# The seam behind the feed-forward stage: where the second tanh, the last gelu and the token outputs stand

## Chip, cores, metric

One core of one Trainium2 chip runs the whole kernel. The metric is the device time in microseconds of one execution; lower is better. TensorE (PE in the rows) multiplies, ScalarE (ACT) evaluates functions, VectorE (DVE) and GpSimd (POOL) do elementwise work, SyncE (SP) issues the DMAs.

## What is computed

64 batches of 256 tokens by 256 features pass through one cross-attention (16 heads of 16, 120 keys) and a coupling network that is applied three times. Cut to what matters:

```python
# attention: query = layernorm(x), key = value = ctx
u = einsum('hbqd,hbkd->hbqk', q, k) * scale / sqrt(d_k)
logits = where(mask, -inf, tanh(u) * exp(log_C))
x = x + (softmax(logits) @ v, heads joined) @ W_out.T

# feed-forward: out = layernorm(x)
gf = global_net(out.mean(axis=1))
for _ in range(3):
    h = gelu(out @ w1 + b1)          # 256 -> 256
    h = gelu(h @ w2 + b2)            # 256 -> 128
    h = gelu(h @ w3 + b3)            # 128 -> 64
    tf = sigmoid(h @ w4 + b4)        # one number per token
    coupling = 0.1 + adaptive_range * (0.7 * gf + 0.3 * tf - 0.5) * 2.0
    out = out + coupling * twist(out)
x = x + out
```

Sigmoids are computed as tanh of half the argument.

## The kernel before

Each engine runs its own program, written out by hand in the order in which it is to run, and waits on semaphores for the others. All of them walk through the same list of stages (`slots()`): attention slots i = -2, -1, 0, ..., and after every eighth batch one feed-forward stage for the eight batches that are then ready (`GROUP` = 8, 8 stages). In attention slot i batches of different age are worked on at once: scores, tanh and exp of batch i; weighted values of batch i-1; queries and keys of batch i+1; the output projection of batch i-2; normalised features of batch i-3 (`LAG` = 3).

Scores and probabilities of a batch come in two halves n = 0 and 1 of eight heads. `scores(b, n)` (L1184) fills four banks of PSUM, `tanh(b, n)` (L939, 120 x 2048 elements) reads them, and the next scores may overwrite them only behind that tanh. `exp(b, n)` (L945) works in place in SBUF; `weighted_values(b, n)` (L1200) multiplies the result with the values.

A feed-forward stage has twelve passes p = 0 to 11 (three cycles of four chunks, two batches to a chunk; `PASSES` = 12, `UPDATES` = 8). A pass is layer 1 and `gelu1` (L973), `layer2` (L1294) and `gelu2` (L997), `layer3` (L1303) and `gelu3` (L1009), and then, in passes 0 to 7, `layer4` and `tanh4`, and in passes 8 to 11 `token_output` (L1334): two columns for each 128 tokens, collected over the four passes. `token_tanh` (L1027) reads the sixteen columns together; `coefficients` on GpSimd (L498) waits for it. `layer3(p)` waits for `gelu3(p-1)`, since all passes use one bank for it.

Eight banks of PSUM: 0 to 3 scores, 4 weighted values, 5 side products, 6 transposes of queries, keys and features (`TR_BANK`), 7 the projection (`X_BANK`). In the feed-forward stage layer 2 uses 4 and 5, and layer 3 uses the first half of bank 6. The token outputs of before lie in bank 6 too, from column 288 (`TOKEN_AT`).

What is called the seam here is the end of a feed-forward stage and the attention slot behind it. Its batch is e = 11, 19, ..., 59 (`early` in the code): seven seams; behind the eighth stage only the end of the program follows. The stage takes work of slot e ahead: TensorE issues `scores(e, 0)` in round p = 10 of its last loop, `scores(e, 1)` in round 11 and `weighted_values(e-1, 0)` in round 12. ScalarE has `tanh(e, 0)` behind `gelu3(9)` and `tanh(e, 1)` behind `gelu3(10)`; `gelu3(11)`, the token tanh, a table load and `exp(e, 0)` follow, then `features(e-3)` (L955), which copies transposed features out of bank 6. In slot e, `queries(e+1)` (L1159) waits for the token tanh, because it overwrites bank 6. On VectorE `attn_out` (L717) transposes weighted values, `queries_out` (L703) and `keys_out` (L708) copy queries and keys out of bank 6, and `residual` (L742) adds the projection.

Each float32 matmul of the code appears in the rows as two MATMULs, so that 8 of them are x16.

## Time and profile before

| what | us |
|---|---|
| median of 3 runs | 1058.44 |
| lowest, highest run | 1058.36, 1059.02 |
| the profiled execution, its own time | 1058.27 |
| its span, from the first to the last instruction | 1056.40 |
| TensorE busy | 974.1 (92%) |
| ScalarE busy | 899.3 (85%) |
| VectorE busy | 818.9 (78%) |
| GpSimd busy | 604.4 (57%) |

The busy shares are averages over stages with different limits. Whether an engine is what the others wait for is read from the idle times before its instructions and from what ended them. All times below count from the start of the span. The rows of a timeline give start, duration, engine, line and operation, what is written and read, how many instructions are merged (x), and, in brackets, the idle time of the engine before the first of them with the instruction that ended it.

### The profile page before, as it was taken

Reading aid. Unit: us, or ns where it says so; the run is one execution under the profiler, and the core shown is the slowest. Engines: PE = TensorE matmul, PEld = TensorE weight load, DVE = VectorE, ACT = ScalarE, POOL = GpSimd, SP = SyncE. Lnnn points to the kernel's source line nnn. Section 1 sums busy time; section 2 is a strip of 40 time slices with the busy share of each in tenths; the row PEclk is TensorE's granted clock in tenths of the full one; section 3 lists DMA queues with packets and bytes.
Section 4 is the critical chain, followed back from the end, with each engine's and each line's share of the span. In section 5 each row is a group of like instructions: output and inputs, shape, how many; then the busy total and the mean of one; then the engine's idle time right before and its main releaser. Section 6 shows DMA issues by size and latency. Waiting matters only on the chain.

```text
span 1056.4 us, 21739 instructions
## 1 busy us (share of the span) xinstructions
PE 974.1 (92%) x7260; PEld 529.3 (50%) x7260; DVE 818.9 (78%) x1655; ACT 899.3 (85%) x1121; POOL 604.4 (57%) x1077
## 2 busy tenths in 40 slices
PE   5899999999999999999999999999999999997993
PEld 4556435564356544565445653556435654454432
DVE  3888785997869876887869978599786887687475
ACT  3899878997899978998789987899789997896575
POOL 3366715887069850898328980588706975087204
PEclk7999999999999999999999999999999999999897
DMA  5433001430023300332005310153002430021002
GB/s 119 89 60 60 6 2 31 118 89 1 2 69 91 78 1 1 90 92 57 2 1 119 89 30 1 30 119 90 0 2 70 94 75 1 1 49 38 11 1 80
DMA packets 191117, 51.70 MB, mean 49 GB/s; under 512 B 165920, under 2 KB 174624, under 8 KB 191008
## 3 DMA queue, kind: packets, MB, share of 16 engines
q1 hardware_dynamic: 191008, 50.31, 22.1%
q8 instruction: 60, 0.98, 0.4%
q14 instruction: 49, 0.40, 0.1%
HBM read 33.37 MB, written 16.78 MB: 47 GB/s over the span
## 4 chain that ended last, share of the span: by engine, by line
PE 46%; ACT 37%; issue 10%; POOL 3%; SPq 2%; DVE 1%; DMA 1%; ACTq 0%; POOLq 0%; DVEq 0%
ACT probs L939 17%; PE ps L1294 15%; ACT probs L945 13%; PE ps L1280 8%; PE ps L1264 6%; PE ps L1303 5%; ACT f_t L955 4%; PE ps L1184 4%; PE ps L1215 3%; PE ps L1200 2%; ACT h L997 1%; PE ps L1324 1%; ACT h L973 1%; PE ps L1334 1%; SPq L412 1%
## 5 line engine op out<-in xcount | busy, mean ns | idle before, releaser
L939 ACT ACTIVATE probs<-ps,u_scale 120x2048 f32<-120x2048 f32 x128 | 258.0, 2015 | 21.2 <-PE ps L1184 20.4
L945 ACT ACTIVATE probs<-probs,exp_bias,clip 120x2048 f32<-120x2048 f32 x128 | 275.6, 2153 | 0.1
L1294 PE MATMUL ps<-h,w 128*128 128x512 f32 x384 | 185.7, 606 | 9.9 <-ACT h L973 8.7
L1184 PE MATMUL ps<-q_t,k_t 32*120 32x256 f32 x2048 | 148.2, 403 | 26.7 <-ACT probs L939 25.9
L717 DVE STREAM_TRANSPOSE o_t<-ps 128x512 f32<-128x512 f32 x128 | 90.6, 708 | 71.5 <-PE ps L1200 71.2
L1215 PE MATMUL ps<-wo_t,of_t 128*128 128x256 f32 x512 | 143.5, 403 | 1.0 <-DVE xy L742 1.0
L498 POOL TENSOR_SCALAR tok_c<-tok_c,c_tok 128x32 f32<-128x32 f32 x8 | 2.3, 288 | 241.6 <-issue 241.6
L1200 PE MATMUL ps<-probs,va 120*32 120x256 f32 x2048 | 138.8, 389 | 1.3 <-ACT probs L945 1.3
L1184 PEld LDWEIGHTS ps<-q_t,k_t 32*120 32x120 f32 x2048 | 93.8, 179 | 63.8 <-issue 59.5
L1215 PEld LDWEIGHTS ps<-wo_t,of_t 128*128 128x128 f32 x512 | 86.9, 189 | 50.0 <-issue 41.7
L1294 PEld LDWEIGHTS ps<-h,w 128*128 128x128 f32 x384 | 67.5, 189 | 87.9 <-issue 58.4
L479 POOL TENSOR_SCALAR f_hat<-xy,neg,rstd 128x256 f32<-128x256 f32 x128 | 102.6, 808 | 13.3 <-POOL rstd L469 13.3
L557 POOL TENSOR_TENSOR f_hl<-f_t,f_hl 128x512 f16<-128x512 f32 x64 | 83.2, 1311 | 35.6 <-DVE f_hl L764 35.6
L973 ACT ACTIVATE h<-f_t,b 128x512 f32<-128x512 f32 x144 | 95.6, 714 | 6.8 <-DVE f_t L827 5.5
L997 ACT ACTIVATE h<-ps,b 128x512 f32<-128x512 f32 x96 | 65.7, 684 | 40.9 <-PE ps L1294 40.9
L458 POOL TENSOR_SCALAR q_hat<-xy,neg,rstd 128x256 f32<-128x256 f32 x128 | 88.1, 696 | 11.0 <-POOL rstd L448 10.5
L1280 PE MATMUL ps<-f_hl,w_hl 128*128 128x512 f16 x384 | 92.6, 385 | 0.0
L802 DVE SCALAR_TENSOR_TENSOR move_u<-coup,r_batch,v_t 128x512 f32<-128x512 f32 x64 | 45.9, 758 | 48.0 <-ACT coup L1021 47.1
L1200 PEld LDWEIGHTS ps<-probs,va 120*32 120x32 f32 x2048 | 53.8, 110 | 56.8 <-ACT probs L945 18.4
L539 POOL TENSOR_SCALAR twisted<-xy,neg,b_r 128x256 f32<-128x256 f32 x112 | 70.5, 637 | 1.2 <-POOL x_add L498 1.1
L1264 PE MATMUL ps<-f_hl,w1t_hl 128*128 128x512 f16 x288 | 68.8, 379 | 0.1
L1303 PE MATMUL ps<-h,w 128*64 128x256 f32 x384 | 62.6, 404 | 3.5
(138 smaller groups left out, 1766.0 us busy)
## 6 DMA issues: line engine op xcount, KB each, us to landing
xy<-in_x_dram SPq DMA_DIRECT2D x64, 256.0 KB, 3.4
out_dram<-xy SPq DMA_DIRECT2D x64, 256.0 KB, 2.0
cbuf<-in_ctx_dram SPq DMA_DIRECT2D x64, 120.0 KB, 2.8
va<-in_ctx_dram SPq DMA_DIRECT2D x64, 120.0 KB, 3.6
tok_c<-coup SPq DMA_DIRECT2D x256, 0.5 KB, 2.0
move_v<-in_L_xattn_W_out_dram SPq DMA_DIRECT2D x1, 256.0 KB, 5.2
move_u<-in_L_ffn_cn_w_dram SPq DMA_DIRECT2D x1, 256.0 KB, 3.3
w<-in_L_ffn_cn_w_dram SPq DMA_DIRECT2D x1, 128.0 KB, 3.1
```

What stands on the lines that cost most here:

```text
L479: eng.tensor_scalar(f_hat[:, t, :], xy[:, at, t * E:(t + 1) * E], neg2[:, at, t:t + 1], rstd2[:, at, t:t + 1], ALU.add, ALU.mult).then_inc ...
L717: eng.transpose(o_t[:, b % 2, 2 * n:2 * n + 2].rearrange("p c q r -> p (c q r)"), banks(PV_BANK)).then_inc(s_ot, 1)
L939: eng.activation(probs[:, b % 2, n * HALF:(n + 1) * HALF, :].rearrange("k h q -> k (h q)"), banks(SCORE_BANK, 4)[0:KEYS, :], ACT.Tanh, sca ...
L945: eng.activation(p, p, ACT.Exp, scale=clip[0:KEYS, 0:1], bias=exp_bias[:, b:b + 1]).then_inc(s_exp, 1)
L973: eng.activation(h1[:, p % 2, m, :], source, ACT.Gelu, bias=b1[:, m:m + 1], scale=by) \
L1184: last = eng.matmul(banks(SCORE_BANK + r)[0:KEYS, odd * S:(odd + 1) * S], k_t[rows, b % 2, odd, n, :], q_t[rows, b % 2, n, :], start=True, ...
L1200: last = eng.matmul(banks(PV_BANK)[j * SLOT:(j + 1) * SLOT, (c % 2) * S:(c % 2 + 1) * S], va[:, b % VR, h, :], probs[:, b % 2, h, :], star ...
L1215: last = eng.matmul(banks(X_BANK)[:, t * E:(t + 1) * E], of_t[:, k, t * P:(t + 1) * P], wo_t[:, k, :], start=(k == 0), stop=(k == EK - 1))
L1264: last = eng.matmul(banks(V_BANKS[m]), w1t_hl[:, w, k, m * P:(m + 1) * P], halves[:, f, k, :], start=(n == 0), stop=(n == len(PRODUCTS) - 1))
L1280: last = eng.matmul(banks(U_BANKS[m]), w1_hl[:, w, k, m * P:(m + 1) * P], halves[:, f, k, :], start=(n == 0), stop=(n == len(PRODUCTS) - 1))
L1294: last = eng.matmul(banks(bank), w2[:, k, :], h1[:, p % 2, k, :], start=(k == 0), stop=(k == EK - 1))
L1303: last = eng.matmul(banks(L3_BANK)[b * M3:(b + 1) * M3, 0:S], w3[:], h2[:, p % 2, b * S:(b + 1) * S], start=True, stop=True, tile_position ...
```

## The change

In the feed-forward stage, ScalarE runs only `tanh(e, 0)` ahead; `tanh(e, 1)` goes into slot e, between `exp(e, 0)` and `features(e-3)`, so `gelu3(11)` stands ahead of it, directly behind `gelu3(10)`. TensorE issues `layer3(11)` ahead of the token outputs of pass 10, and moves `scores(e, 1)` and `weighted_values(e-1, 0)` from the stage into slot e. The token outputs lie in bank 7 at column 0. `queries(e+1)` waits for `gelu3(11)` instead of the token tanh, and the projection in slot e waits for the token tanh instead of the last `tanh4`. Slot e on TensorE has another order, and on VectorE it begins with `queries_out(e+1)`. Slots other than e keep their order.

```diff
-        TOKEN_AT = S + 32
+        TOKEN_BANK = X_BANK
...
+                    if after_ffn(i) and nxt < NB:
+                        queries_out(nxt)
                     if 0 <= here < NB:
                         attn_out(here, 0)
-                    if 0 <= nxt < NB:
+                    if 0 <= nxt < NB and not after_ffn(i):
                         queries_out(nxt)
...
                     if 0 <= i < NB:
                         exp(i, 0)
+                    if i < NB and first:
+                        tanh(i, 1)
...
                             gelu3(i, p - 1)
-                            if early < NB and p >= PASSES - 2 and p < PASSES:
-                                tanh(early, p - PASSES + 2)
+                            if early < NB and p == PASSES - 2:
+                                tanh(early, 0)
...
                 elif after_ffn(b - 1):
-                    eng.wait_ge(s_ttok, groups_before(b - 1))
+                    eng.wait_ge(s_h3, PASSES * groups_before(b - 1))
...
                     if after_ffn(b + 2):
-                        eng.wait_ge(s_th, UPDATES * groups_before(b + 2))
+                        eng.wait_ge(s_ttok, groups_before(b + 2))
...
-                    at = TOKEN_AT + t * GROUP + chunk * CB
-                    last = eng.matmul(banks(TR_BANK)[:, at:at + CB], h3[:, p % 2, t * P:(t + 1) * P],
+                    at = t * GROUP + chunk * CB
+                    last = eng.matmul(banks(TOKEN_BANK)[:, at:at + CB], h3[:, p % 2, t * P:(t + 1) * P],
...
-                        if p - 2 >= UPDATES:
+                        if p - 2 >= UPDATES and p < PASSES:
                             token_output(i, p - 2)
                         if p - 1 < PASSES:
                             layer3(i, p - 1)
+                        if p >= PASSES:
+                            token_output(i, p - 2)
...
-                        if early < NB:
-                            if p == PASSES - 2:
-                                scores(early, 0)
-                            if p == PASSES - 1:
-                                scores(early, 1)
-                            if p == PASSES:
-                                weighted_values(early - 1, 0)
+                        if early < NB and p == PASSES - 2:
+                            scores(early, 0)
```

TensorE at the first seam, before. `h` is the output of a gelu, L1294 layer 2, L1303 layer 3, L1334 the token outputs of one pass, L1184 scores, L1200 weighted values, L1215 projection, L1159 queries, L1168 keys, L1228 features:

```order
L1294 MATMUL ps<-h,w 128x512 x2
L1334 MATMUL ps<-w4rep,h 128x2 x2
L1303 MATMUL ps<-h,w 64x256 x2
L1184 MATMUL ps<-q_t,k_t 120x256 x8
L1334 MATMUL ps<-w4rep,h 128x2 x2
L1303 MATMUL ps<-h,w 64x256 x2
L1200 MATMUL ps<-probs,va 32x256 x8
L1334 MATMUL ps<-w4rep,h 128x2 x2
L1215 MATMUL ps<-wo_t,of_t 128x256 x2
L1159 MATMUL ps<-ident,q_hat 128x128 x4
L1200 MATMUL ps<-probs,va 32x256 x8
L1168 MATMUL ps<-ident,cbuf 128x120 x2
```

Behind these come the second projection, the features and the scores of batch e+1. The same place on TensorE in the changed kernel, whose lines stand 4 further down (L1298 is layer 2, L1307 layer 3, L1338 token outputs, L1188 scores, L1204 weighted values, L1219 projection, L1163 queries, L1172 keys, L1232 features):

```order
L1298 MATMUL ps<-h,w 128x512 x2
L1338 MATMUL ps<-w4rep,h 128x2 x2
L1307 MATMUL ps<-h,w 64x256 x4
L1338 MATMUL ps<-w4rep,h 128x2 x4
L1188 MATMUL ps<-q_t,k_t 120x256 x8
L1163 MATMUL ps<-ident,q_hat 128x128 x4
L1204 MATMUL ps<-probs,va 32x256 x8
L1172 MATMUL ps<-ident,cbuf 128x120 x2
L1219 MATMUL ps<-wo_t,of_t 128x256 x2
L1204 MATMUL ps<-probs,va 32x256 x8
L1232 MATMUL ps<-ident,f_hat 128x128 x4
L1219 MATMUL ps<-wo_t,of_t 128x256 x2
```

The two layer 3 stand together, and so do the last two token outputs; a block of scores and one of weighted values have moved from ahead of the last token outputs to behind them.

ScalarE at the same seam, before (L997 is gelu2, L1009 gelu3, L939 tanh, L945 exp, L1027 the token tanh, L955 features):

```order
L939 ACTIVATE probs<-ps,u_scale 120x2048
L997 ACTIVATE h<-ps,b 128x512
L1009 ACTIVATE h<-ps,b 128x256
L939 ACTIVATE probs<-ps,u_scale 120x2048
L1009 ACTIVATE h<-ps,b 128x256
L1027 ACTIVATE tok_th<-ps,half_b 128x16
L945 ACT_TABLE_LOAD
L945 ACTIVATE probs<-probs,exp_bias,clip 120x2048
L955 ACTIVATE f_t,f_sum<-ps 128x256 x2
L939 ACTIVATE probs<-ps,u_scale 120x2048
```

And in the changed kernel, where each of these lines stands 2 further down:

```order
L941 ACTIVATE probs<-ps,u_scale 120x2048
L999 ACTIVATE h<-ps,b 128x512
L1011 ACTIVATE h<-ps,b 128x256 x2
L1029 ACTIVATE tok_th<-ps,half_b 128x16
L947 ACT_TABLE_LOAD
L947 ACTIVATE probs<-probs,exp_bias,clip 120x2048
L941 ACTIVATE probs<-ps,u_scale 120x2048
L957 ACTIVATE f_t,f_sum<-ps 128x256 x2
L941 ACTIVATE probs<-ps,u_scale 120x2048
```

The second tanh has moved from between the last two gelus to behind the exp.

## Rows read from the trace of the kernel before

**Rows 1.** The page: shares of the chain that ended last, by engine, by line.

```profile
PE 46%; ACT 37%; issue 10%; POOL 3%; SPq 2%; DVE 1%; DMA 1%; ACTq 0%; POOLq 0%; DVEq 0%
ACT probs L939 17%; PE ps L1294 15%; ACT probs L945 13%; PE ps L1280 8%; PE ps L1264 6%; PE ps L1303 5%; ACT f_t L955 4%; PE ps L1184 4%; PE ps L1215 3%; PE ps L1200 2%; ACT h L997 1%; PE ps L1324 1%; ACT h L973 1%; PE ps L1334 1%; SPq L412 1%
```

**Rows 2.** Waits of ScalarE, 171.9 to 297.3 us: us in total, times, longest us.

```profile
ACT probs L939 <- PE ps L1184: 0.9, 2, 0.6
```

**Rows 3.** Timeline of ScalarE, first seam: start, duration, instruction, idle before.

```profile
167.47 0.47 ACT L1009 ACTIVATE h<-ps,b 128x256 f32<-128x256 f32 x1 [0.24 <-PE ps L1303]
168.56 1.97 ACT L939 ACTIVATE probs<-ps,u_scale 120x2048 f32<-120x2048 f32 x1 [0.61 <-PE ps L1184]
170.43 0.47 ACT L1009 ACTIVATE h<-ps,b 128x256 f32<-128x256 f32 x1
171.59 0.27 ACT L1027 ACTIVATE tok_th<-ps,half_b 128x16 f32<-128x16 f32 x1 [0.70 <-PE ps L1334]
...
173.18 2.10 ACT L945 ACTIVATE probs<-probs,exp_bias,clip 120x2048 f32<-120x2048 f32 x1
...
176.92 1.97 ACT L939 ACTIVATE probs<-ps,u_scale 120x2048 f32<-120x2048 f32 x1 [0.26 <-PE ps L1184]
178.79 2.08 ACT L945 ACTIVATE probs<-probs,exp_bias,clip 120x2048 f32<-120x2048 f32 x1
```

**Rows 4.** Timeline of TensorE, the same stretch.

```profile
166.77 0.65 PE L1303 MATMUL ps<-h,w 128*64 128x256 f32 x4
167.35 1.14 PE L1184 MATMUL ps<-q_t,k_t 32*120 32x256 f32 x16
...
170.95 0.61 PE L1334 MATMUL ps<-w4rep,h 128*128 128x2 f32 x4 [0.33 <-ACT h L1009]
171.41 1.11 PE L1215 MATMUL ps<-wo_t,of_t 128*128 128x256 f32 x4
172.36 0.60 PE L1159 MATMUL ps<-ident,q_hat 128*128 128x128 f32 x4
172.89 1.07 PE L1200 MATMUL ps<-probs,va 120*32 120x256 f32 x16
173.89 0.42 PE L1168 MATMUL ps<-ident,cbuf 120*128 120x120 f32 x2
174.15 1.03 PE L1215 MATMUL ps<-wo_t,of_t 128*128 128x256 f32 x4
175.16 0.63 PE L1228 MATMUL ps<-ident,f_hat 128*128 128x128 f32 x4
175.71 1.14 PE L1184 MATMUL ps<-q_t,k_t 32*120 32x256 f32 x16
```

**Rows 5.** Timeline of ScalarE, second seam: the tanh of the next slot.

```profile
302.42 1.97 ACT L939 ACTIVATE probs<-ps,u_scale 120x2048 f32<-120x2048 f32 x1 [0.26 <-PE ps L1184]
```

**Rows 6.** Timeline of all engines, end of the eighth feed-forward stage.

```profile
1038.44 0.47 ACT L1009 ACTIVATE h<-ps,b 128x256 f32<-128x256 f32 x1 [0.24 <-PE ps L1303]
...
1038.97 0.61 PE L1334 MATMUL ps<-w4rep,h 128*128 128x2 f32 x4 [0.57 <-ACT h L1009]
...
1039.50 0.65 PE L1303 MATMUL ps<-h,w 128*64 128x256 f32 x4
1040.20 0.47 ACT L1009 ACTIVATE h<-ps,b 128x256 f32<-128x256 f32 x1 [1.29 <-PE ps L1303]
...
1040.73 1.01 PE L1334 MATMUL ps<-w4rep,h 128*128 128x2 f32 x4 [0.57 <-ACT h L1009]
1041.78 0.27 ACT L1027 ACTIVATE tok_th<-ps,half_b 128x16 f32<-128x16 f32 x1 [1.10 <-PE ps L1334]
```

**Rows 7.** Timeline of VectorE, first seam: the copy of the queries.

```profile
173.00 0.69 DVE L703 COPY q_t<-ps 128x512 f32<-128x512 f32 x1 [1.60 <-PE ps L1159]
```

**Rows 8.** Windows in the tail: PEclk is the granted clock as a share.

```profile
1040.20:1040.60 0.40, 0.00 (x0) 0.00 (x0) 0.00 (x0) 0.40 (x1) 0.00 (x0) 0.95 0.00 0
1040.60:1041.00 0.40, 0.27 (x2) 0.27 (x2) 0.00 (x0) 0.08 (x1) 0.00 (x0) 0.50 0.00 0
```

More of the change, by code:

```diff
@@ L1026, in token_tanh @@
                 eng.wait_ge(s_coef, COEFS * g)
-                eng.activation(tok_th[:], banks(TR_BANK)[:, TOKEN_AT:TOKEN_AT + GT], ACT.Tanh, scale=0.5,
+                eng.activation(tok_th[:], banks(TOKEN_BANK)[:, 0:GT], ACT.Tanh, scale=0.5,
                                bias=half_b4[:, 0:1]).then_inc(s_ttok, 1)
@@ L1371, in _ @@
                             project(old, 0)
-                    else:
-                        if old < NB:
-                            project(old, 0)
+                        if 0 <= nxt < NB:
+                            keys(nxt)
+                        if 0 <= here < NB:
+                            weighted_values(here, 1)
+                        if 0 <= old < NB:
+                            project(old, 1)
+                        if 0 <= i - LAG < NB:
+                            norm_to_features(i - LAG)
+                    else:
+                        if i < NB:
+                            scores(i, 1)
                         if nxt < NB:
@@ L1377, in _ @@
                         if here < NB:
-                            weighted_values(here, 1)
-                    if 0 <= nxt < NB:
-                        keys(nxt)
-                    if 0 <= here < NB and i != early:
-                        weighted_values(here, 1)
-                    if 0 <= old < NB:
-                        project(old, 1)
-                    if 0 <= i - LAG < NB:
+                            weighted_values(here, 0)
+                        if nxt < NB:
+                            keys(nxt)
+                        if old < NB:
+                            project(old, 0)
+                        if here < NB:
+                            weighted_values(here, 1)
                         norm_to_features(i - LAG)
+                        if old < NB:
+                            project(old, 1)
                     if i == 0:
```

## The prediction

> **What bounds the kernel now.** I read the page's chain of waits first. TensorE holds 46% of it and ScalarE 37%, and the two largest single lines of it are the tanh and the matmuls of layer 2 [rows 1]. In the stretch between two seams (from behind the token tanh of the first to the one of the second) ScalarE waits for scores only twice, 0.9 us in all [rows 2]. One attention slot after another therefore runs from one ACTIVATE to the next: whatever moves the start of tanh(e+1,0), the first tanh of the slot behind the seam, moves everything after it. Here e is the batch whose scores the feed-forward stage takes ahead: 11, 19, ... 59, so there are seven seams; the eighth stage has none.
>
> So I look at what sets that tanh. In the timeline of ScalarE across the first seam there are idle times of 0.24, 0.61, 0.70 and 0.26 us in the rows shown, each ended by TensorE [rows 3]. The last, before tanh(12,0) at 176.92, was ended by the scores of batch 12, whose matmuls began at 175.71. In the timeline of TensorE these stand at the end of an unbroken file: token outputs at 170.95, which had waited 0.33 us for the last gelu, then projection, queries, weighted values, keys, projection, features, scores [rows 4]. That file is the path; the exp and the table load on ScalarE lie beside it. In the second seam the same tanh starts at 302.42, which is 125.50 us later, one whole group of eight batches; the seams repeat [rows 5].
>
> **The change part by part: the tanh and its scores.** Before, tanh(e,1) stood between gelu3(10) and gelu3(11). It started at 168.56, so the last gelu couldn't run before 170.43 [rows 3]. That tanh is now behind exp(e,0), and its scores (1.07 us of TensorE, 167.35 to 168.42) behind the last token outputs [rows 4]. The last layer 3 no longer has to follow scores and token outputs. It waits for gelu3(10), because that gelu reads the same bank. Gelu3(10) started at 167.47 [rows 3]; from the start of such a gelu to the TensorE instruction that waits for it are 0.53 us (1038.44 to 1038.97, in the tail) [rows 6]. So layer3(11) starts at 168.00. From its start to the start of its gelu are 0.70 us where TensorE had just worked (166.77 to 167.47, 1039.50 to 1040.20) [rows 3, 4, 6]. Here it comes out of an idle time of 0.58 us (layer3(10) began at 166.77 and took 0.65). Token outputs behind an idle time handed over after 0.53 us (1038.97 to 1039.50), those behind work after at most 0.47; so I add 0.05, between nothing and 0.10, and have gelu3(11) start at 168.75. Token outputs of pass 11 then start 0.53 later at 169.28, against 170.95: 1.67 us earlier. The token tanh follows 0.64 later (170.95 to 171.59) at 169.92, also 1.67 earlier.
>
> The Trainium skill has a rule on that addition: the page TensorE: Matmul & The Clock Gate, section "Single matmul latency", says that an isolated matmul shows its drain while one in a stream hides it. By that rule the 0.70 would be 0.80 here, and the sum 0.05 us a seam higher than mine; the token rows agree in direction (0.53 against 0.47).
>
> **TensorE behind the token outputs.** Before, the file from 170.95 to the scores at 175.71 was 4.76 us. The new file has all of it, plus two blocks that used to lie in the shadow of ScalarE's tanh: scores(e,1), 1.07 us, and weighted_values(e-1,0). The latter's price is that of its twin, 172.89 to 173.89, 1.00 us. Step by step, start to start [rows 4]: token outputs 0.46, scores 1.07, queries 0.53, weighted values 1.00, keys 0.26, projection 0.98 (0.95 and 1.01 are there), weighted values 1.00, features 0.55, projection 0.98. The sum is 6.83 us. 169.28 + 6.83 = 176.11, against 175.71: the scores of batch 12 start 0.40 us **later**, and tanh(12,0) with them, at 177.32. The gain of 1.67 us at the token outputs is eaten by 2.07 us of matmuls that lost their cover. Six of the junctions (such as features to projection) don't occur in the trace; the junctions that do differ by a few hundredths, so I allow 0.10 us either way.
>
> What else lies in the file's way: queries need their bank free, and that is now told by gelu3(11), over at about 169.2, before their 170.81. Keys need the queries' copy on VectorE: 0.64 us after the start of the queries (172.36 to 173.00) plus its 0.69 [rows 4, 7], so 172.14, against the keys' turn at 172.34. That is 0.20 us of slack, and it is there because the copy now goes ahead of the transpose of o_t. Projection waits for the token tanh, which is long over. ScalarE: exp at 171.51 (1.59 behind the token tanh, as before, with a table load between), tanh(11,1) at 173.61 if the exp takes its 2.10, its end at 175.58 [rows 3]. The scores of 12 overwrite its banks and must wait for it, and TensorE gets there at 176.11: 0.5 us of slack. So TensorE's file is still what comes last. The coefficients on GpSimd start 1.67 us earlier, and VectorE's queue is less crowded, but neither ends a wait of tanh(12,0); nothing is taken from that.
>
> **The tail.** The eighth stage has no scores in it, only layer3(11) in front of token outputs(10). Before: 1038.97, 1039.50, gelu 1040.20, token outputs 1040.73, token tanh 1041.78 [rows 6]. Now layer3(11) starts at 1038.97, gelu3(11) at 1039.72, token outputs at 1040.25. Their way to the tanh is 0.64 us at 2.4 GHz (the seam) and 1.05 us at 1.2 GHz (1040.73 to 1041.78); the clock fell between 1040.2 and 1040.6 [rows 8]. So the token tanh comes at 1040.89 or 1041.30, 0.89 or 0.48 us earlier. I take 0.7. The chain behind it (coefficients, twisted parts, stores) is unchanged.
>
> **The sum.** 7 x 0.40 = 2.8, less 0.7, is +2.1 us. With the allowances (7 x 0.10 and 0.2 for the tail) it is +1.2 to +3.0. The profiled execution took 1058.27 us, of which 1056.40 is its span; the median of the runs is 1058.44, 0.17 above. On the profile's own time the sum gives 1060.4, on the median 1060.5.
>
> **Rivals.** (1) ScalarE's order becomes the path and the gain is kept. If TensorE's blocks pack closer than the rows show, scores(12,0) wait for tanh(11,1) alone. With an exp step of 2.00 (its 2.10 less the 0.10 by which a tanh overlaps the next ACTIVATE, 176.92 + 1.97 against 178.79 [rows 3]) that ends at 175.48, scores 0.05 later, 0.2 us before the old 175.71. Then 7 x -0.2 and the tail's -0.7 give -2.1: 1056.3. Against it: 0.5 us would have to vanish from nine steps read in this same seam.
> (2) TensorE's clock falls in the seam: slower. The seam now looks like the tail: behind the last layer 2 come only a layer 3, an idle time of half a microsecond, a layer 3, and token outputs of two columns, and in the tail the clock fell from 2.4 to 1.2 GHz behind exactly such a sequence, with no idle time of the matmuls over 0.57 us [rows 6, 8]. Before, scores and weighted values stood between them. The token outputs took 1.05 instead of 0.64 us there, a factor of 1.6. If a third to a half of the file's 6.8 us meets the low clock, at a price of 0.6 of its time, a seam that is hit pays 1.4 to 2.0, say 1.5 us. It decides from the first seam hit in seven: one makes 1062.0, two make 1063.5. The Trainium skill, same page, section "HAM oscillation — how this bites in real kernels", blames stretches in which the engine waits idle for data, much longer than any gap here; by that rule no seam would fall and this rival would be void. The tail speaks against the rule.
> (3) The slack of 0.20 us at the keys, or the wait of features for k_t, isn't there: VectorE's copy and transpose come late by contention with GpSimd's coefficients, which now run at the same time. Then each seam costs 0.2 to 0.4 more, +3.5 to +4.9: about 1062.6.
> (4) The change doesn't do what it says: the last gelu stays where it was, at 170.43, held by another wait. Then the file starts at 170.95 as before with 6.83 instead of 4.76 us in it, 7 x 2.07 = 14.5 us, 1072.2 with the tail's gain. Its waits are for layer 3 and for a token output long done, so I see no holder.
>
> **How the numbers follow.** The forecast gets 0.60, split at 0.2% (2.1 us, about what a measurement of this kernel can tell from no change). I put 0.33 of the 0.60 within and 0.27 above. Rival 1: 0.10, half faster, half same. Rival 2: 0.18, rival 3: 0.10, rival 4: 0.02, all slower. Faster 0.05, same 0.33 + 0.05 = 0.38, slower 0.27 + 0.30 = 0.57. The likeliest value stands almost on the border. The likeliest case's own range is 1059.6 to 1061.4; for 8 times in 10 I take 1058.0 to 1063.0.
>
> **What would show it.** In the changed profile: the last gelu3 at 168.75 and the token tanh at 169.92 in the first seam (right if the freed gelu is right); the scores of batch 12 at 176.1 straight behind a projection, without idle time before them (right if TensorE's file is the bound; an idle time ended by the tanh would mean rival 1); tanh(12,0) at 177.3; the second seam 0.8 us late in all, the seventh 2.8; the token tanh of the last stage at 2.1 more than 1041.78. A granted clock of 0.5 anywhere in a seam would be rival 2, an idle TensorE before keys or features rival 3. I would be wrong at the root if ScalarE, not TensorE, ended the wait of tanh(12,0).

## The result and the profile after

The changed kernel takes 1063.62 us (median of 16 runs, 1061.76 to 1072.12) against 1059.26 us of the kernel before on the same chip (16 runs, 1057.30 to 1059.83). The ratio is 1.0055, with a 95% interval of 1.0042 to 1.0068: slower. The medians lie 4.4 us apart and the means, of which the ratio is made, 5.8 us. The forecast was 1060.5 and the range ended at 1063.0. The spread has grown from 2.5 to 10 us. The profiled execution took 1063.60 us, with a span of 1061.8.

The timeline of ScalarE across the first seam, to be laid beside [rows 3] (start, duration, line, idle time before and what ended it):

```profile
167.64 0.47 ACT L1011 ACTIVATE h<-ps,b 128x256 f32<-128x256 f32 x1 [0.24 <-PE ps L1307]
168.90 0.47 ACT L1011 ACTIVATE h<-ps,b 128x256 f32<-128x256 f32 x1 [0.79 <-PE ps L1307]
170.07 0.27 ACT L1029 ACTIVATE tok_th<-ps,half_b 128x16 f32<-128x16 f32 x1 [0.70 <-PE ps L1338]
...
171.66 2.10 ACT L947 ACTIVATE probs<-probs,exp_bias,clip 120x2048 f32<-120x2048 f32 x1
173.66 1.95 ACT L941 ACTIVATE probs<-ps,u_scale 120x2048 f32<-120x2048 f32 x1
...
177.51 1.97 ACT L941 ACTIVATE probs<-ps,u_scale 120x2048 f32<-120x2048 f32 x1 [1.13 <-PE ps L1188]
```

And of TensorE, beside [rows 4]:

```profile
166.94 0.65 PE L1307 MATMUL ps<-h,w 128*64 128x256 f32 x4
168.21 0.65 PE L1307 MATMUL ps<-h,w 128*64 128x256 f32 x4 [0.62 <-issue]
168.79 1.24 PE L1338 MATMUL ps<-w4rep,h 128*128 128x2 f32 x8
169.96 1.14 PE L1188 MATMUL ps<-q_t,k_t 32*120 32x256 f32 x16
171.03 0.66 PE L1163 MATMUL ps<-ident,q_hat 128*128 128x128 f32 x4
171.62 1.07 PE L1204 MATMUL ps<-probs,va 120*32 120x256 f32 x16
172.62 0.42 PE L1172 MATMUL ps<-ident,cbuf 120*128 120x120 f32 x2
172.88 1.03 PE L1219 MATMUL ps<-wo_t,of_t 128*128 128x256 f32 x4
173.85 1.07 PE L1204 MATMUL ps<-probs,va 120*32 120x256 f32 x16
174.85 0.66 PE L1232 MATMUL ps<-ident,f_hat 128*128 128x128 f32 x4
175.34 1.03 PE L1219 MATMUL ps<-wo_t,of_t 128*128 128x256 f32 x4
176.30 1.14 PE L1188 MATMUL ps<-q_t,k_t 32*120 32x256 f32 x16
```

This execution came to the seam 0.17 us late (layer3(10) at 166.94 against 166.77). With that taken off, the token tanh starts at 169.90 instead of 171.59, as intended. But TensorE then works through an unbroken file up to the scores of batch 12, which start at 176.13 (again less the 0.17), against 175.71. The tanh of batch 12 has waited 1.13 us for them; it was 0.26 before.

The second seam runs the same code, but it looks different. Windows of TensorE's granted clock (the columns are the stretch, its length, busy time of each engine with the number of instructions, PEclk, DMA share, GB/s), and then its timeline:

```profile
295.00:296.00 1.00, 0.97 (x8) 0.87 (x7) 0.00 (x0) 0.29 (x1) 0.00 (x0) 0.84 0.06 16
296.00:297.00 1.00, 1.00 (x9) 0.82 (x12) 0.00 (x0) 0.88 (x2) 0.43 (x2) 0.50 0.00 0
...
299.00:300.00 1.00, 1.00 (x17) 0.41 (x16) 0.69 (x1) 1.00 (x2) 1.00 (x3) 0.95 0.00 0
```

```profile
294.12 0.65 PE L1307 MATMUL ps<-h,w 128*64 128x256 f32 x4 [0.62 <-issue]
294.70 1.36 PE L1338 MATMUL ps<-w4rep,h 128*128 128x2 f32 x8
296.00 2.08 PE L1188 MATMUL ps<-q_t,k_t 32*120 32x256 f32 x16
298.00 1.11 PE L1163 MATMUL ps<-ident,q_hat 128*128 128x128 f32 x4
...
303.73 1.14 PE L1188 MATMUL ps<-q_t,k_t 32*120 32x256 f32 x16
```

PEclk 0.50 is 1.2 GHz, 1.00 is 2.4 GHz. The clock fell at 295.7 us, within the last token outputs (294.70, 1.36 us, against 1.24 in the first seam), and stayed down for 3.4 us. The block of scores took 2.00 us start to start, where it takes 1.07 in the first seam, and the queries 1.05 instead of 0.59. The table says how much later than in the kernel before the first tanh of batch e+1 starts, as the step that each seam adds (from the timelines of ScalarE of the two profiled executions, each seam against the one ahead of it, the first less the 0.17 us):

| seam | 1 | 2 | 3 | 4 | 5 | 6 | 7 |
|---|---|---|---|---|---|---|---|
| changed kernel, us | 0.41 | **1.92** | 0.42 | 0.42 | 0.42 | **2.00** | 0.41 |

The bold ones are the seams with a granted clock below 1.00. Between the seams nothing is added. The sum is 7 x 0.42 = 2.9 for the longer file and 3.1 for the two falls. The end of the program gives back 0.76: the shift is 6.19 us at the last seam and 5.43 at the last token tanh (1047.21 against 1041.78). The rest, 0.2, came ahead of the first seam.

The tail, beside [rows 6]:

```profile
1044.57 0.47 ACT L1011 ACTIVATE h<-ps,b 128x256 f32<-128x256 f32 x1 [0.24 <-PE ps L1307]
...
1045.14 0.65 PE L1307 MATMUL ps<-h,w 128*64 128x256 f32 x4 [0.62 <-issue]
...
1045.72 1.45 PE L1338 MATMUL ps<-w4rep,h 128*128 128x2 f32 x8
1045.83 0.47 ACT L1011 ACTIVATE h<-ps,b 128x256 f32<-128x256 f32 x1 [0.79 <-PE ps L1307]
1047.21 0.27 ACT L1029 ACTIVATE tok_th<-ps,half_b 128x16 f32<-128x16 f32 x1 [0.90 <-PE ps L1338]
```

From the start of gelu3(10) to the token tanh of the eighth stage are 2.64 us (1044.57 to 1047.21), where they were 3.34 (1038.44 to 1041.78): 0.70 us less. Of these, 0.50 lie between the two gelus (1.26 us against 1.76) and so come from the new order.

### The profile page after: what moved, and what is told of

The parts are those of the page before. It is cut to its first block, busy times and chain, and to the rows that moved or that the text cites. A ratio compares the mean times of both kernels' runs of the same rounds, so it can differ in the third digit from the quotient of the medians.

```text
span 1061.8 us, 21739 instructions
## 1 busy us (share of the span) xinstructions
PE 976.7 (92%) x7260; PEld 531.4 (50%) x7260; DVE 819.9 (77%) x1655; ACT 898.9 (85%) x1121; POOL 600.1 (57%) x1077
## 4 chain that ended last, share of the span: by engine, by line
PE 47%; ACT 37%; issue 9%; POOL 3%; SPq 2%; DVE 1%; DMA 1%; ACTq 0%; POOLq 0%; DVEq 0%
ACT probs L941 17%; PE ps L1298 15%; ACT probs L947 13%; PE ps L1284 8%; PE ps L1268 5%; PE ps L1307 5%; ACT f_t L957 4%; PE ps L1188 3%; PE ps L1219 2%; PE ps L1204 2%; ACT h L999 1%; PE ps L1338 1%; PE ps L1328 1%; SPq L412 1%; ACT h L975 1%
## 5 line engine op out<-in xcount | busy, mean ns | idle before, releaser
L1298 PE MATMUL ps<-h,w 128*128 128x512 f32 x384 | 185.7, 606 | 9.9 <-ACT h L975 8.7
L1188 PE MATMUL ps<-q_t,k_t 32*120 32x256 f32 x2048 | 151.1, 409 | 27.3 <-ACT probs L941 26.3
L1219 PE MATMUL ps<-wo_t,of_t 128*128 128x256 f32 x512 | 143.0, 402 | 1.0 <-DVE xy L742 1.0
L1204 PE MATMUL ps<-probs,va 120*32 120x256 f32 x2048 | 138.4, 388 | 1.9 <-ACT probs L947 1.9
L1188 PEld LDWEIGHTS ps<-q_t,k_t 32*120 32x120 f32 x2048 | 95.6, 182 | 63.1 <-issue 58.5
L1219 PEld LDWEIGHTS ps<-wo_t,of_t 128*128 128x128 f32 x512 | 86.9, 189 | 50.0 <-issue 41.7
L1298 PEld LDWEIGHTS ps<-h,w 128*128 128x128 f32 x384 | 67.5, 189 | 87.9 <-issue 58.4
L703 DVE COPY q_t<-ps 128x512 f32<-128x512 f32 x64 | 42.1, 658 | 67.3 <-PE ps L1163 67.3
L1204 PEld LDWEIGHTS ps<-probs,va 120*32 120x32 f32 x2048 | 53.9, 110 | 57.6 <-ACT probs L947 20.7
L1307 PE MATMUL ps<-h,w 128*64 128x256 f32 x384 | 62.6, 404 | 8.4 <-issue 5.0
```

What stands on the lines that cost most here:

```text
L1188: last = eng.matmul(banks(SCORE_BANK + r)[0:KEYS, odd * S:(odd + 1) * S], k_t[rows, b % 2, odd, n, :], q_t[rows, b % 2, n, :], start=True, ...
L1204: last = eng.matmul(banks(PV_BANK)[j * SLOT:(j + 1) * SLOT, (c % 2) * S:(c % 2 + 1) * S], va[:, b % VR, h, :], probs[:, b % 2, h, :], star ...
L1219: last = eng.matmul(banks(X_BANK)[:, t * E:(t + 1) * E], of_t[:, k, t * P:(t + 1) * P], wo_t[:, k, :], start=(k == 0), stop=(k == EK - 1))
L1298: last = eng.matmul(banks(bank), w2[:, k, :], h1[:, p % 2, k, :], start=(k == 0), stop=(k == EK - 1))
L1307: last = eng.matmul(banks(L3_BANK)[b * M3:(b + 1) * M3, 0:S], w3[:], h2[:, p % 2, b * S:(b + 1) * S], start=True, stop=True, tile_position ...
```

## Experiments

Two questions were open: is the longer file on TensorE the steady part of the loss, and do the falls of the clock come from how sparse the seam has become? Ratios below are against the kernel before, run beside each on the same chip (medians 1058.34, 1058.33 and 1058.09 us in the three groups).

**The changed kernel again** (no edit).

> The changed kernel once more, unaltered, as the base for the others. Theory (0.40 us per seam from TensorE's longer file, and in some executions TensorE's clock falling in one to several seams at 1.5 us each): every execution at 1060.3 plus a whole number of 1.5 us steps, median 1062 to 1064, spread 2 us and more, and in the profile each seam of +0.4 or, with a granted clock of 0.5 in it, +1.9. Rival (contention somewhere in the slots, the same in every execution): about the same time in every execution, and the extra spread evenly over seams and slots.

1066.20 us (6 runs, 1062.96 to 1071.85), ratio 1.0076 (1.0056 to 1.0096). Its steps are 0.42, 0.39, 0.41, 0.41, **3.54**, **1.98**, 0.24. Windows of the fifth seam:

```profile
672.00:676.00 4.00, 3.35 (x26) 2.58 (x28) 0.00 (x0) 2.12 (x4) 0.65 (x3) 0.78 0.00 0
676.00:680.00 4.00, 4.00 (x30) 1.74 (x27) 0.93 (x2) 3.99 (x3) 3.82 (x12) 0.50 0.00 0
680.00:684.00 4.00, 4.00 (x32) 2.52 (x31) 2.21 (x5) 1.12 (x5) 1.52 (x3) 0.87 0.01 4
```

The clock was down from 674.2 to 681.1 here, twice as long as in any other fall within a seam, and it cost 3.1 us over the steady 0.4; the sixth seam paid 1.57. So 4 of the 14 seams of these two profiled executions had a fall, none outside a seam between the 50th microsecond and the end of the last seam. (Behind the last seam, as the attention slots run out, the clock falls for 6.8 us in every profile, that of the kernel before at 975.7 us included.) I had expected times in whole steps of 1.5 us. They are not so tidy, since the start of the program varies by some 2 us of its own (below), but they do go with the mean granted clock: of the 22 runs of this and the first measurement, the three with a clock of 0.983 are at 1061.8 to 1062.2, the eleven with 0.977 to 0.980 at 1062.8 to 1065.7, the five with 0.975 to 0.976 at 1066.2 to 1066.6, the three with 0.972 at 1071.2 to 1072.1.

**A filler in the sparse stretch.**

```diff
                             layer3(i, p - 1)
+                        if early < NB and p == PASSES - 1:
+                            eng.wait_ge(s_h2, PASSES * i + p)
+                            eng.matmul(banks(PV_BANK)[:, 0:S], ident[:], wo_t[:, 0, :], start=True, stop=True)
                         if p >= PASSES:
                             token_output(i, p - 2)
```

> The changed kernel with one more matmul (128x256 float32, 0.48 us, its product is overwritten unread) in each seam, in TensorE's idle 0.6 us between the last two layer 3. It adds no step to the file. Theory of the clock: the sparse stretch is filled, the clock doesn't fall in the seams any more, every seam is +0.4, all executions lie within 1 us around 1061, 1.5 to 3 us below the median of the unaltered one. Rival (the falls have nothing to do with how sparse the seam is, or the extra is contention): same time and same spread as the unaltered changed kernel, or 0.1 us per seam more.

1060.79 us (7 runs, 1060.15 to 1062.29), ratio 1.0024 (1.0014 to 1.0035): 5.4 us below the unaltered changed kernel beside it, by adding work. Against the 16 runs of the first measurement it is 3.3 us by the two ratios. TensorE in the first seam:

```profile
166.98 0.65 PE L1307 MATMUL ps<-h,w 128*64 128x256 f32 x4
167.56 0.70 PE L1446 MATMUL ps<-wo_t,ident 128*128 128x256 f32 x2
168.25 0.65 PE L1307 MATMUL ps<-h,w 128*64 128x256 f32 x4
168.83 1.24 PE L1338 MATMUL ps<-w4rep,h 128*128 128x2 f32 x8
```

The filler (L1446, its two passes) ends where the last layer 3 may start, so the path is as long as in the changed kernel: the steps of its seams are 0.4 each (0.24 at the last, since this execution had made up 0.17 us on the way to it). The windows of two of its seven seams; the other five read 1.00 too:

```profile
292.00:306.00 14.00, 13.38 (x134) 8.24 (x136) 6.83 (x15) 11.11 (x14) 7.21 (x19) 1.00 0.00 1
...
670.00:684.00 14.00, 13.38 (x141) 8.25 (x139) 7.34 (x16) 11.11 (x14) 7.73 (x19) 1.00 0.00 1
```

**The same matmul elsewhere**, behind the scores of e, where TensorE has no idle time.

```diff
                         if i < NB:
                             scores(i, 1)
+                        eng.matmul(banks(PV_BANK)[:, 0:S], ident[:], wo_t[:, 0, :], start=True, stop=True)
                         if nxt < NB:
                             queries(nxt)
```

> The control of the filler: the same added matmul (128x256 float32), not in the idle time between the last two layer 3, but behind the scores of e in slot e, where TensorE is busy anyway. Theory (it is the sparse stretch that lets the clock fall): falls and spread as in the unaltered changed kernel, and each seam 0.5 us later still, since the matmul lies in the file: 7 x 0.5 = 3.4 us more, 1065 to 1070. Rival (any added matmul in the seam, or another place in the trace, does what the filler did): 1061 to 1064.5 with no fall.

1065.29 us (4 runs, 1063.70 to 1066.13), ratio 1.0064 (1.0050 to 1.0078). The steps are **2.49**, 0.88, 0.90, 0.90, 0.90, 0.91, 0.89: each seam has 0.48 more than the changed kernel, the duration of the matmul on the path, and the first has a fall besides:

```profile
166.00:170.00 4.00, 3.35 (x26) 2.18 (x28) 0.00 (x0) 2.27 (x5) 0.00 (x0) 0.97 0.01 2
170.00:174.00 4.00, 4.00 (x34) 2.53 (x38) 0.37 (x1) 3.97 (x4) 3.45 (x12) 0.61 0.00 0
```

So an added matmul doesn't keep the clock up by itself. That this place does less for it than the idle gap is shown only by one fall in seven seams against none in seven; in four runs the falls were fewer than I expected. The steady part, 7 x 0.9 = 6.3 us, is most of the 7.2 us between it and the kernel before.

**The second tanh alone.** The kernel before with only ScalarE's order changed.

```diff
+                    if i < NB and first:
+                        tanh(i, 1)
...
-                            if early < NB and p >= PASSES - 2 and p < PASSES:
-                                tanh(early, p - PASSES + 2)
+                            if early < NB and p == PASSES - 2:
+                                tanh(early, 0)
```

> The kernel before with one part of the change: tanh(e,1) goes behind exp(e,0) on ScalarE, so that the last gelu runs first; TensorE's and VectorE's orders and the bank stay. Theory (worked out on the seam of before): token outputs 0.4 us earlier, TensorE's file not longer, but the scores of e+1 now wait for tanh(e,1), which ends at 176.7, and start 1.1 us later than 175.71, a wait ended by ScalarE: 7 x 1.1 = 7.6 us, about 1066, with no fall of the clock. Rival (moving the tanh is free or a gain as long as TensorE has no more to do): 1055 to 1059.

1066.22 us (4 runs, 1065.33 to 1066.91), ratio 1.0071 (1.0057 to 1.0085). TensorE waits 1.48 us, and what ends the wait is the tanh; the steps of its seams are 1.1 (0.95 at the last), as worked out:

```profile
175.79 0.63 PE L1230 MATMUL ps<-ident,f_hat 128*128 128x128 f32 x4
177.90 1.14 PE L1186 MATMUL ps<-q_t,k_t 32*120 32x256 f32 x16 [1.48 <-ACT probs L939]
```

The clock didn't fall in any of its seams. Here TensorE's file is short, and ScalarE's order is the path. In the changed kernel the file is long and covers that wait. The two limits stand close together, which the next run measures.

**Projection 1 out of the file.** The changed kernel with the second half of the projection moved behind the first scores of e+1.

```diff
                         if 0 <= i < NB:
                             scores(i, 0)
+                        if after_ffn(i - 1):
+                            project(i - 3, 1)
...
                         norm_to_features(i - LAG)
-                        if old < NB:
-                            project(old, 1)
```

> The changed kernel, but the second half of the projection of batch e-2 goes behind the first scores of batch e+1 (0.97 us out of the file ahead of them). Theory (TensorE's file is the bound, ScalarE's own order comes 0.5 us behind it): the scores start 0.5 to 0.6 us earlier, not 0.97, their wait is now ended by tanh(e,1), and the time is 7 x 0.55 = 3.9 us below the unaltered changed kernel in undisturbed executions. Rival (the path runs elsewhere, over VectorE or GpSimd): no gain, or a loss since the residual comes later.

1064.29 us (6 runs, 1063.51 to 1069.21), ratio 1.0072 (1.0053 to 1.0091): no gain in the end, although its first half came as foreseen. TensorE and VectorE in the first seam and the slot behind it:

```profile
175.56 1.14 PE L1188 MATMUL ps<-q_t,k_t 32*120 32x256 f32 x16 [0.24 <-ACT probs L941]
176.63 1.13 PE L1219 MATMUL ps<-wo_t,of_t 128*128 128x256 f32 x4
...
182.16 0.40 PE L1172 MATMUL ps<-ident,cbuf 120*128 120x120 f32 x2 [0.69 <-DVE q_t L703]
```

```profile
177.87 0.71 DVE L737 STREAM_TRANSPOSE of_t<-o_n 128x512 f32<-128x512 f32 x1 [0.81 <-PE ps L1219]
...
180.07 0.40 DVE L837 TENSOR_TENSOR xy<-xy,twisted 128x256 f32<-128x256 f32 x1
...
181.36 0.65 DVE L703 COPY q_t<-ps 128x512 f32<-128x512 f32 x1
```

The scores start 0.24 us after TensorE is free, released by the tanh, and the tanh of batch 12 starts 0.6 us earlier than in the changed kernel. One slot later the keys wait 0.69 us for the queries' copy on VectorE (181.36). That copy stands in a queue behind of_t, which waited 0.81 us for the moved projection, and behind a combine (180.07). The step of a seam is -0.17 us at the first tanh of e+1 and +0.86 at that of e+2. Its profiled execution has no fall in a seam; two of its runs, at 1069.1 and 1069.2, have a lower mean clock (0.978 against 0.980 to 0.982).

**A new order on the kernel before.** ScalarE's order and the early scores of before; token outputs in bank 7; on TensorE in slot e: queries, weighted values, keys, projection 0, features, the scores of e+1, and only then projection 1.

```diff
                     else:
-                        if old < NB:
-                            project(old, 0)
                         if nxt < NB:
                             queries(nxt)
                         if here < NB:
                             weighted_values(here, 1)
+                        if nxt < NB:
+                            keys(nxt)
+                        if old < NB:
+                            project(old, 0)
```

> The kernel before with its order on ScalarE (second tanh ahead of the last gelu) and its scores and weighted values inside the stage, but token outputs in the other bank, and on TensorE in slot e: queries, weighted values, keys, projection 0, features, then scores of batch e+1, then projection 1. Theory (TensorE's file from the last token outputs to those scores is the path in the kernel before too): it shrinks from 4.76 to about 3.8 us, tanh(e+1,0) starts 0.8 to 0.9 us earlier, 7 x 0.85 = 6 us: 1052.5 to 1053.5. Rival (other waits come last at once, such as the copy of the keys): 0 to 3 us gained.

1059.80 us (11 runs, 1057.99 to 1060.28), ratio 1.0008 (0.9999 to 1.0016): nothing gained, so the rival was the nearer one, and its 0 to 3 us are missed too if the 0.9 us by the ratio are a loss, which these runs don't settle. The gain is there at the first tanh of e+1, 0.95 us, and at the first of e+2 it is gone (+0.08), in the way of the run above. There too the keys wait 0.69 us for the queries' copy. The diff leaves out the bank and the late projection, which are as in the changed kernel and in the run above, and the conditions that keep slot e from issuing the moved blocks twice.

**The same with a later combine**, and with the tail's swap.

```diff
                     if not after_ffn(i):
                         for b in late[:1]:
                             combine(b)
+                    if after_ffn(i - 1):
+                        late = late[1:]
...
-                    if after_ffn(i):
+                    if after_ffn(i - 1):
                         for b in late[:1]:
                             combine(b)
-                    late = late[1:]
+                    if not after_ffn(i):
+                        late = late[1:]
```

> The new order on TensorE (as in the run before, with projection 1 behind the scores of e+1), the tail's swap, and on VectorE the first combine moved from the end of slot e to behind the queries' copy of slot e+1, the second to that slot's end. In the new order alone the gain of 0.85 us per seam was lost one slot later, where the keys waited 0.7 us on TensorE for the queries' copy, queued behind that combine. Theory: with the copy out of that queue the gain stays: 7 x 0.85 + 0.7 = 6.6 us, 1051.5 to 1053. Rival (the projection's later result, through the residual and the features, costs it anyway): 1056.5 to 1058.

1055.27 us (5 runs, 1053.58 to 1055.55), ratio 0.9962 (0.9950 to 0.9975). This is faster than both kernels, but by less than I had worked out (3.1 us by the medians, 4.0 by the ratio, of 6.6). Each seam gives 0.91 us at the first tanh of e+1, and 0.36 are returned in that slot, where TensorE, with the projection in its file, comes to the scores of e+2 a quarter of a microsecond late (the last row). Over seven seams the steps sum to 3.8 us.

In the timeline of ScalarE the tanh of batch 12 follows the features without an idle time, and that of batch 13 waits:

```profile
177.17 1.97 ACT L942 ACTIVATE probs<-ps,u_scale 120x2048 f32<-120x2048 f32 x1
...
185.93 1.97 ACT L942 ACTIVATE probs<-ps,u_scale 120x2048 f32<-120x2048 f32 x1 [0.24 <-PE ps L1187]
```

**The changed kernel with all repairs**: filler, late projection, later combine.

> The changed kernel with all three repairs: the filler, projection 1 behind the first scores of e+1, and the first combine behind the next slot's copy of the queries. Theory: no falls of the clock; tanh(e+1,0) ends up 0.3 us earlier than in the kernel before, and 0.36 us are given back one slot later by TensorE, which has the projection in its file there (as in the new order with the later combine); the tail gives 0.7: 1057 to 1058, still 2 us above the new order built on the kernel before, because its scores wait for tanh(e,1). Rival (the order on ScalarE costs nothing once the rest is repaired): 1054 to 1055.5.

1058.63 us (11 runs, 1058.08 to 1060.22), ratio 1.0006 (0.9997 to 1.0015). The edits are the three shown above, together. The first tanh of e+1 comes about 0.15 us earlier per seam than in the kernel before, against 0.91 in the run above, and no seam has a fall. The 0.76 us a seam between them (5.3 us in all; 4.7 by the two ratios) is the price of having the scores of e+1 wait for a tanh behind the exp: TensorE idles 0.25 us ahead of them in the first seam, until that tanh ends. I had put the gain at 0.3 us per seam and the time at 1057 to 1058.

**The queries' copy behind the weighted values.** The changed kernel with VectorE's order of before in slot e.

```diff
-                    if after_ffn(i) and nxt < NB:
-                        queries_out(nxt)
                     if 0 <= here < NB:
                         attn_out(here, 0)
-                    if 0 <= nxt < NB and not after_ffn(i):
+                    if 0 <= nxt < NB:
                         queries_out(nxt)
```

> The changed kernel without one part: on VectorE in slot e the transpose of the weighted values goes ahead of the queries' copy again. Theory (the keys on TensorE had only 0.2 to 0.3 us of slack behind that copy): the copy starts at 173.4 instead of 171.7, the keys wait 1.5 us with an idle TensorE, and the first scores of e+1 start 1.5 us later per seam, 7 x 1.5 = 10.3 us over the undisturbed changed kernel: 1070 to 1074. Rival (the copy's place is immaterial): as the unaltered changed kernel.

1079.19 us (4 runs, 1079.09 to 1079.55), ratio 1.0195 (1.0181 to 1.0209). The keys wait as foreseen:

```profile
172.72 1.07 PE L1202 MATMUL ps<-probs,va 120*32 120x256 f32 x16
175.30 0.40 PE L1170 MATMUL ps<-ident,cbuf 120*128 120x120 f32 x2 [1.51 <-DVE q_t L703]
```

The steps of its seams are 1.98, **3.56**, **3.39**, 1.96, **3.53**, 1.96, **3.37**. So the wait costs 1.55 us a seam over the changed kernel, 10.8 in all, as foreseen. The four bold seams have a fall of the clock (at 298.6, 428.3, 684.3 and 940.3 us), 6.0 us together, more than I had allowed. All four began between 0.0 and 0.8 us behind the token tanh, while the 1.51 us at the keys begin 2.6 us behind it or later: that idle time did not bring them on.

**Token outputs ahead of layer3(11).** The changed kernel with TensorE's order of before at that place.

```diff
-                        if p - 2 >= UPDATES and p < PASSES:
+                        if p - 2 >= UPDATES:
                             token_output(i, p - 2)
                         if p - 1 < PASSES:
                             layer3(i, p - 1)
-                        if p >= PASSES:
-                            token_output(i, p - 2)
```

> The changed kernel without one part: the token outputs of pass 10 go ahead of layer3(11) again, in all eight stages. Theory (layer3(11) is on the path from gelu3(10) on, token outputs take 0.53 us): the last gelu 0.53 us later, TensorE's file of 0.54 us less behind it once token outputs(10) are gone from there, but the file begins with token outputs(11), which wait for that gelu: every seam 0.5 us later than in the changed kernel, 7 x 0.5 + 0.7 in the tail = 4.2 us more without falls of the clock, 1065 to 1068 with them. Rival (their order is immaterial since TensorE has the same work): as the changed kernel.

1068.98 us (4 runs, 1066.38 to 1074.12), ratio 1.0107 (1.0080 to 1.0134). The profiled execution, 1066.38 us, had no fall in a seam, and its steps are 0.90 to 0.92: 0.50 more than the changed kernel's. The swap of these two is worth 0.5 us a seam, as worked out. Two of the other runs, at 1071.1 and 1074.1, have mean clocks of 0.975 and 0.972 and lie above what I expected.

**The tail alone.** The kernel before, with layer3(11) ahead of token outputs(10) in the eighth stage only, whose token outputs lie in bank 7.

```diff
+                        swap = p == PASSES and early >= NB
-                        if p - 2 >= UPDATES:
+                        if p - 2 >= UPDATES and not swap:
                             token_output(i, p - 2)
                         if p - 1 < PASSES:
                             layer3(i, p - 1)
+                        if swap:
+                            token_output(i, p - 2)
```

> The kernel before with the tail's part of the change alone: in the eighth stage layer3(11) goes ahead of the token outputs of pass 10, which lie in bank 7 there. Theory: the last token tanh 0.5 to 0.9 us earlier, everything ahead of it unchanged: 0.5 to 0.9 us below the kernel before. Rival (the end is set by something else, stores or GpSimd): no change.

1057.65 us (median of 11 runs), ratio 0.9994 (0.9984 to 1.0003). Ten of the runs lie at 1057.02 to 1059.19; one took 3226.05 us, for a reason that no profile shows, and the ratio leaves it out. The last token tanh starts at 1040.91 instead of 1041.78, of which 0.16 came with the start of the program. The times agree with the remaining 0.7 us but can't tell it from nothing. The timeline of ScalarE can:

```profile
1038.48 0.47 ACT L1009 ACTIVATE h<-ps,b 128x256 f32<-128x256 f32 x1 [0.24 <-PE ps L1303]
1039.74 0.47 ACT L1009 ACTIVATE h<-ps,b 128x256 f32<-128x256 f32 x1 [0.79 <-PE ps L1303]
1040.91 0.27 ACT L1027 ACTIVATE tok_th<-ps,half_b 128x16 f32<-128x16 f32 x1 [0.70 <-PE ps L1334]
```

The last gelu follows gelu3(10) after 1.26 us instead of 1.76. So it does in the tail of every profile with this swap, and in none without it: 0.50 us are the swap's. The way from gelu3(10) to the token tanh is 2.43 us here against 3.34; the other 0.41 is the clock, which stayed up until the token outputs were nearly done. The kernel with token outputs ahead of layer3(11), without the swap, has 1.76 us between the gelus and the same 0.41 us less behind them (2.93 in all), with a clock that fell only behind the token tanh.

## Why the prediction was wrong

- **The freed gelu and the token tanh: right.** Predicted 168.75 and 169.92, measured (less the 0.17 of this execution) 168.73 and 169.90.
- **The allowance of 0.05 us for a layer 3 out of an idle time: wrong, and made up for by luck.** From layer3(11) to its gelu are 0.69 us (168.21 to 168.90), as behind work. The start of layer 3 behind the gelu took 0.57 instead of 0.53 and hid the error. The reading behind the allowance was wrong too: the 0.53 us from token outputs to the layer 3 behind them don't come from an idle time, since in the first seam of before they are 0.54 right behind scores (168.42 to 168.96), and the token outputs that did come out of an idle time, at 170.95, handed over after 0.46. The Trainium skill says that a single isolated matmul can't hide its drain (TensorE: Matmul & The Clock Gate, "Step-by-step: what each phase is for"); these rows show no difference between the layer 3 behind 0.62 us of idle time and one behind work, and the 0.80 us of the prediction was not reached. The two rows of TensorE before, behind scores that began at 167.35:

```profile
168.42 0.61 PE L1334 MATMUL ps<-w4rep,h 128*128 128x2 f32 x4
168.96 0.65 PE L1303 MATMUL ps<-h,w 128*64 128x256 f32 x4
```

- **TensorE's file: right.** The last eight of its nine steps sum to 6.37 us, and from the start of the scores of e (169.96) to those of batch 12 (176.30) are 6.34. Single steps were off by up to 0.06, in both directions (queries to weighted values 0.59 for 0.53, features to projection 0.49 for 0.55). The step of a seam is 0.42 us where 0.40 stood.
- **The slack of 0.2 us at the keys: right.** The copy was over at 172.42 (171.73 and 0.69) and the keys followed without a pause at 172.62; with the copy one place further back they waited 1.51 us.

```profile
171.73 0.69 DVE L703 COPY q_t<-ps 128x512 f32<-128x512 f32 x1 [8.73 <-PE ps L1163]
```

- **ScalarE 0.5 us behind as the next limit: right at the seam.** With the projection out of the way the tanh ended the wait, 0.24 us after TensorE was free.
- **The tail: right.** It gave 0.70 us from gelu3(10) to the token tanh where 0.7 stood: 0.50 by the swap, and 0.20 because the clock fell later than before. In executions whose clock stays up it is 0.91, close to the upper one of the two values worked out, 0.48 and 0.89; that this one came out in the middle is luck.
- **Rival 2, the fall of the clock: here the prediction failed.** The sum has no term for a fall, the rival got a chance of 0.18, and the range ended at 1063.0, although two falls were worked out at 1063.5. In the two profiled executions of the changed kernel there were two falls each, worth 3.1 us in the first, and the runs' times and mean clocks say that most executions have some. I had the sequence of matmuls from [rows 6] in front of me, had said that it was followed by a fall in the tail, and then treated seven repetitions of it in the seams as a rare accident. The 4.4 us between the medians are the steady 2.2 (2.9 less the tail) and one to two falls.
- **The price of a fall: right by luck.** It is 1.5 to 1.6 us in this kernel (3.1 for the long one), as against 1.5. But I had 2.3 to 3.4 us of the file's work at a price of 0.6 of its time. In the second seam the 3.4 us of low clock held only some 1.9 us of such work (3.4 less the 1.5 lost), at a price of 0.8: scores 2.00 for 1.07, queries 1.05 for 0.59. The 0.6 came from the way of token outputs to their tanh (1.05 for 0.64), and scores take a larger factor.
- **What bears out the cause of the falls.** With the filler the sum without a fall comes out (+2.45 us by the medians, +2.1 worked out), and none of the 14 seams in the two profiles with a filler in the gap has a fall. All 18 runs of these two kernels have a mean clock of 0.982 to 0.985, as against 3 of the 22 of the unaltered changed kernel. The control is weaker: with the same matmul elsewhere, one seam in seven fell, and two of four runs have 0.982 or more, so it isn't shown that only the gap will do.

The Trainium skill's section "HAM oscillation — how this bites in real kernels" (same page) speaks of long idle stretches of the engine. Here the longest idle time of the matmuls in the changed kernel's seams ahead of a fall is 0.62 us, so it is no safe guide for this seam; the runs decide against it.

## What to carry to other kernels

When an instruction is moved off a waiting engine's path, list the work that was lying under its cover; here 2.07 us of matmuls ate a gain of 1.67 us. If a rival is a thing that can happen at every one of n repetitions, its chance is that of n trials, and the range has to reach at least one or two hits. A price that comes out right should be taken apart as well: here the share of work hit was too high and the factor too low. A matmul whose result nobody reads, put where TensorE would idle anyway, can be worth microseconds (3.3 to 5.4 here); on the path the same matmul cost 0.48 us a seam.

## What was unexpected of the hardware

- The granted clock fell from 2.4 to 1.2 GHz in seams in which TensorE was idle for no more than 0.62 us at a stretch; what went ahead were two layer 3 and token outputs of two columns. Of the nine falls in seams that the profiles hold, eight lasted 3.4 us and one 6.8.
- The two profiled executions of the changed kernel differ by 1.2 us ahead of the first seam already (tanh(11,0) at 164.82 and 165.99). In the profile of the kernel with token outputs first, this tanh was 2.5 us later than in the profile of before. The clock changes its level several times in the first 50 us of every trace. The spread of the kernel before is of that size, 2.5 us; that the one explains the other wasn't tried.
- How much the last stage's tail takes depends on where the clock falls in it: the token outputs of pass 11 reach their tanh in 0.64 us or in 1.05.
- Left open: why some executions of the changed kernel took 1071 to 1072 us. None of them was profiled, but their mean clock was the lowest, 0.972 against 0.978 in the profiled one with two falls. As an estimate, 0.006 less over 1070 us is 13 us more at the half clock, or about four more falls of 3.4 us, at 1.5 to 1.6 us each some 6 us more than its 1063.6; the start varies by up to 2.5 us. So these may be executions in which most seams had a fall.
